# Query and key stacks loaded one head at a time, projections spread between score units, and modulation rows summed on GpSimd

## The reference

```
mod0 = silu(L0_c) @ L0_wmod          # (1,512) @ (512, 3072): shift, scale, gate of each half block
mod1 = silu(L1_c) @ L1_wmod          # the same for block 1
h  = layernorm(x) * (1 + scale) + shift
q  = (h @ Wq.T) -> 32 heads of 16;  k, v = (h @ Wk.T), (h @ Wv.T) -> 8 heads of 16
q, k = rope(q), rope(k)
s  = q k^T / 4, causal over 1024 tokens;  out = softmax(s) @ v;  x = x + gate * (out @ Wo.T)
# then: mlp with top-2 routing, a mixer block, a gated mlp with low-rank terms, each with shift, scale, gate
```

## Time and profile before

| | us |
|---|---|
| median of 3 runs | 860.44 (856.64 to 864.11) |
| the profiled execution | 860.34 |
| its span in the trace | 858.5 |
| mean granted TensorE clock | 0.952 of full |

### The profile page before, as it was taken

The page is one execution under the profiler, slowest core; times in us unless marked ns, Lnnn a source line. Parts: engine busy times, 40 slices in busy tenths (PEclk is TensorE's granted clock), DMA queues, the critical chain, the costliest instruction groups (busy, mean ns, idle before and its releaser), DMA issues.

```text
span 858.5 us, 11485 instructions
## 1 busy us (share of the span) xinstructions
PE 757.5 (88%) x3902; PEld 454.3 (53%) x3902; DVE 471.0 (55%) x714; ACT 322.1 (38%) x532; POOL 204.8 (24%) x158
## 2 busy tenths in 40 slices
PE   5979489999999999979889999877778899997998
PEld 2434233243333433217658888634336688885886
DVE  4636556667667677406855637693686423336310
ACT  6311056555665556771315500253213222322100
POOL 1405560200000000161246513231323122222500
PEclk9979789999999999999999999998779899999999
DMA  9291994510010100211014300110221011111110
GB/s 316 71 147 15 170 175 119 73 63 25 38 62 0 62 28 36 90 38 62 2 29 106 98 1 0 39 54 1 36 54 49 24 50 49 49 31 43 62 62 37
DMA packets 24376, 52.88 MB, mean 62 GB/s; under 512 B 4017, under 2 KB 8857, under 8 KB 23321
## 3 DMA queue, kind: packets, MB, share of 16 engines
q1 hardware_dynamic: 24345, 52.46, 23.6%
HBM read 45.63 MB, written 6.62 MB: 61 GB/s over the span
## 4 chain that ended last, share of the span: by engine, by line
PE 74%; DVE 10%; issue 5%; DMA 4%; ACT 3%; SPq 2%; POOL 2%; ACTq 0%; DVEq 0%; POOLq 0%
PE ps L842 72%; DVE mxp L1691 2%; DMA Qst<-mparts 1%; ACT pr L1395 1%; DVE xnb L1588 1%; PE ps L859 1%; DMA q_parts<-qparts 1%; DMA x<-in_x 1%; DVE st L1566 1%; PE ps L997 1%; DMA Qst<-q_parts 1%; DVE arena L1595 1%; DVE dg L1922 1%; DVE rt L1880 1%; SPq L717 1%
## 5 line engine op out<-in xcount | busy, mean ns | idle before, releaser
L842 PE MATMUL ps<-arena 128*128 128x512 f32 (+1 forms) x1416 | 333.6, 397 | 12.9 <-ACT full L1522 5.4
L842 PEld LDWEIGHTS ps<-arena 128*128 128x128 f32 (+1 forms) x1416 | 266.4, 189 | 74.3 <-DVE arena L1598 11.7
L1691 DVE TENSOR_REDUCE mxp<-ps 128x2 f32<-128x1024 f32 (+3 forms) x160 | 173.2, 1115 | 83.7 <-PE ps L842 83.0
L1395 ACT ACTIVATE pr<-ps 128x512 f32<-128x512 f32 x288 | 161.7, 596 | 126.6 <-PE ps L842 123.9
L842 PE MATMUL ps<-Qst,Kst 99*128 (+1 forms) x288 | 105.7, 388 | 16.8 <-DMA Qst<-mparts 9.4
L842 PE MATMUL ps<-Kst,Qst 96*128 (+4 forms) x384 | 102.7, 340 | 10.0 <-DMA Qst<-q_parts 5.8
L842 PE MATMUL ps<-pr,vr 128*32 128x512 f32 x576 | 77.6, 611 | 0.7 <-ACT pr L1395 0.7
L842 PE MATMUL ps<-maskb,identb 128*128 128x128 bf16 (+1 forms) x320 | 76.2, 260 | 0.0
L842 PEld LDWEIGHTS ps<-Kst,Qst 96*128 (+1 forms) x384 | 37.0, 101 | 73.1 <-issue 40.7
L842 PEld LDWEIGHTS ps<-Qst,Kst 99*128 (+1 forms) x288 | 27.2, 97 | 86.6 <-ACT pr L1395 48.9
L2097 POOL COPY vr<-vtok 128x128 f32 (+1 forms) x8 | 2.3, 291 | 206.1 <-PE ps L842 206.1
(11 more groups left out here) (187 smaller groups left out, 786.0 us busy)
## 6 DMA issues: line engine op xcount, KB each, us to landing
wmr<-in_wmr SPq DMA_DIRECT2D x8, 1280.0 KB, 6.0
raw<-in_w SPq DMA_DIRECT2D x16, 512.0 KB, 3.3
Qst<-q_parts SPq DMA_DIRECT2D x18, 256.0 KB, 8.8
q_parts<-qparts SPq DMA_DIRECT2D x3, 768.0 KB, 8.4
x<-in_x SPq DMA_DIRECT2D x8, 256.0 KB, 6.3
wm<-in_wm SPq DMA_DIRECT2D x4, 512.0 KB, 7.1
raw<-in_up SPq DMA_DIRECT2D x8, 256.0 KB, 2.6
raw<-in_down SPq DMA_DIRECT2D x8, 256.0 KB, 2.6
```

The lines of the kernel that those rows point to most:

```text
L842: return nc.tensor.matmul(outp, lhs, rhs, start=start, stop=stop, skip_group_check=True)
L1395: A(pr[:, k % PRING, :], ps[:, 4 + k % 2, :], ACT.Exp, scale=float(DH) ** -0.5).then_inc(exp_done, 1)
L1691: V.tensor_reduce(mxp[:, kh, g0:g0 + heads, i].rearrange("p (b e) -> p b e", e=per), units, AXX, ALU.max)\
```

## The change

- `Qst` and `Kst` hold three heads instead of eight; head h uses slot h % 3. Nine DMAs load a head: three for the keys (one for each group of rows), six for the queries (64 KB for a half, 128 KB for all tokens). Head h+2's are issued after head h's maxima rows and, from h = 1, after head h-1's transposed units are all done.
- SyncE's order is one plain list: maxima rows of head h, its modulation row, next weights, then (h < 3) the store of query parts h+1, then the loads of head h+2. The first modulation weights are loaded in the front.
- The first queries are projected before the second half of the layer norm is turned. The splitting of the first queries moves to VectorE; the keys' stays on ScalarE, VectorE and GpSimd.
- Values of the second half and query groups 1 and 2 are projected in halves, one behind each of the first ten score units; the transposes of the values follow unit 11, group 3 stands around the first maxima and head 1's first units.
- GpSimd weighs the four chunks of a modulation piece by the conditioning (a number for each partition) and adds them to `wsum`; `mod_step` is then four products with ones.
- The loops over heads are written out on all engines.

```diff
+    if n >= NKV - 2:
         return slots_before(NKV) + 2 * (n - (NKV - 2))
     return slots_before(n + 2, "ctx")
+
+
+FILL = (("v", 1), ("q", 1, 0), ("q", 1, 1), ("q", 2, 0), ("q", 2, 1))
+VT_AT = 11
...
+            sp.dma_start(wmr[:, :, :].rearrange("p c n -> p (c n)"), a["wmr"][0]).then_inc(wmr_in, 16)
+
+            def load_keys(n, tok_, done):
+
+                for r0, parts_ in ((0, 3), (3, 2), (5, 1)):
+                    sp.dma_start(Kst[DH * r0:DH * (r0 + parts_), n % 3, tok_], kscr[0:parts_, DH * n:DH * n + DH, tok_])\
+                        .then_inc(done, 16)
...
+            def load_queries(n, tok_, done):
+
+                r = G * DH * (n % 2)
+                for k, part in enumerate(Q_PARTS):
+                    sp.dma_start(Qst[DH * k:DH * k + DH, n % 3, :, tok_],
+                                 qscr[n // 2, part, r:r + G * DH, tok_].rearrange("(g d) t -> d g t", d=DH)).then_inc(done, 16)
...
-            load_keys(2, NKV, slice(0, T), k_rest)
...
-            def later_queries(c):
-
-                sp.wait_ge(part_q, c)
-                sp.dma_start(qscr[c, :, :, :].rearrange("q p t -> p q t"), qparts[:, :, :]).then_inc(q_out, 16)
-                sp.wait_ge(q_out, 16 * c)
-                load_queries(c, slice(0, T), q_in[c])
...
+                sp.wait_ge(k_lo, hf + 1)
+                sp.dma_start(kscr[:, :, tok[hf]].rearrange("q p t -> p q t"), parts[2 * hf][:, :, :]).then_inc(part_out[2 * hf], 16)
+                sp.wait_ge(q_lo, hf + 1)
+                sp.dma_start(qscr[0, :, :, tok[hf]].rearrange("q p t -> p q t"), parts[2 * hf + 1][:, :, :])\
+                    .then_inc(part_out[2 * hf + 1], 16)
+                sp.wait_ge(part_out[2 * hf], 16)
+                load_keys(0, tok[hf], s0_in[hf])
+                sp.wait_ge(part_out[2 * hf + 1], 16)
+                load_queries(0, tok[hf], s0_in[hf])
+            load_keys(1, every, st_in[1])
+            load_queries(1, every, st_in[1])
+            sp.dma_start(lraw[:, :], a["lora"]).then_inc(lraw_in, 16)
...
                 sp.wait_ge(s_read, slots_before(h, NS + 1) + 1)
-                for blk in range(2):
-                    sp.dma_start(mscr[blk, bass.ds(h * MODW, MODW)].rearrange("(q n) -> q n", n=MODW // 4),
-                                 full[16 * blk:16 * blk + 97:32, 0, 0:MODW // 4]).then_inc(modrow_out, 16)
-                if more:
-                    sp.wait_ge(s_full, slots_before(h, NS + 1) + 1)
-                    sp.dma_start(wmr[:, :, :].rearrange("p c n -> p (c n)"),
-                                 a["wmr"][bass.ds(h + 1, 1)].rearrange("o p n -> (o p) n")).then_inc(wmr_in, 16)
-
-            head_dmas(0, True)
-            later_queries(2)
-            head_dmas(1, True)
-            later_queries(3)
-            sp.dma_start(lraw[:, :], a["lora"]).then_inc(lraw_in, 16)
-            with sp.Fori(0, NKV - 3) as k:
...
-            sp.wait_ge(modrow_out, 32 * NKV)
+                sp.dma_start(mscr[h * MODW:(h + 1) * MODW].rearrange("(q n) -> q n", n=MODW // 4), full[0:97:32, 0, 0:MODW // 4])\
+                    .then_inc(modrow_out, 16)
+                if h < NKV - 1:
+                    sp.wait_ge(wsum_ready, h + 1)
+                    sp.dma_start(wmr[:, :, :].rearrange("p c n -> p (c n)"), a["wmr"][h + 1]).then_inc(wmr_in, 16)
+
+            for h in range(NKV):
+                head_dmas(h)
+                if h < 3:
+                    sp.wait_ge(part_q, h + 1)
+                    sp.dma_start(qscr[h + 1, :, :, :].rearrange("q p t -> p q t"), qparts[:, :, :]).then_inc(q_out, 16)
+                if h < NKV - 2:
+
+                    sp.wait_ge(q_out, 16 * ((h + 2) // 2))
+                    if h:
+                        sp.wait_ge(t_full, h * NTU)
+                    load_keys(h + 2, every, st_in[h + 2])
+                    load_queries(h + 2, every, st_in[h + 2])
...
             pe.wait_ge(wkv_in, 16)
             keys(0)
-            ln_turn(0, 1)
             pe.wait_ge(wq_sorted, KC)
             queries(0, 0)
+            ln_turn(0, 1)
             keys(1)
             queries(0, 1)
             values(0)
-            queries(1, 0)
...
-                pe.wait_ge(wmr_in, 16 * h + 16)
-
+                pe.wait_ge(wsum_ready, h + 1)
                 w = MODW // 4
-                for kc in range(KC):
-                    for q in range(4):
-                        last = mm(ps[32 * q:32 * q + 32, 2, 0:w], sc32[:, kc, :, :].rearrange("p l m -> p (l m)"),
-                                  wmr[:, kc, w * q:w * q + w], kc == 0, kc == KC - 1)
+                for q in range(4):
+                    last = mm(ps[32 * q:32 * q + 32, 2, 0:w], ones[:, 0:32], wsum[:, w * q:w * q + w], True, True)
                 last.then_inc(s_full, 1)
...
+            pe.wait_ge(s0_in[0], 144)
             for s in range(NS):
                 if s == LATER:
-                    values(1)
-                    queries(1, 1)
+                    pe.wait_ge(s0_in[1], 144)
+                s_unit(0, s)
+                if s < 2 * len(FILL):
+
+                    job, half = FILL[s // 2], range(2 * (s % 2), 2 * (s % 2) + 2)
+                    if job[0] == "v":
+                        values(job[1], half)
+                    else:
+                        queries(*job[1:], half)
+                if s == VT_AT:
                     for hf in range(2):
                         values_turn(hf)
-                    pe.wait_ge(k_in[1], 96)
-                    pe.wait_ge(q0_in[1], 96)
-                s_unit(0, s)
-                if s in (7, 10, 13, 16):
-                    queries(*divmod((7, 10, 13, 16).index(s) + 4, 2))
             max_turn(0)
+            queries(3, 0)
             mod_step(0)
+            pe.wait_ge(st_in[1], 144)
             for s in range(AHEAD):
                 s_unit(1, s)
+                if s in (1, 3):
+                    queries(3, 1, range(s - 1, s + 1))
...
-            head_body(0, True, True, False)
-            with pe.Fori(0, NKV - 3) as k:
-                head_body(k + 1, True, True, True)
-            head_body(NKV - 2, True, False, True)
-            head_body(NKV - 1, False, False, True)
+            for n in range(NKV):
+                head_body(n, n < NKV - 1, n < NKV - 2, n > 0)
...
+                n = 2 * hf + 1
+                dve.wait_ge(rope_q, n + 1)
+                V.tensor_copy(parts[n][:, 0, :], rq[n][:, :]).then_inc(q_part, 1)
+                dve.wait_ge(q_part, 3 * hf + 1)
+                V.tensor_tensor(rq[n][:, :], rq[n][:, :], parts[n][:, 0, :], ALU.subtract).then_inc(q_part, 1)
+                dve.wait_ge(q_part, 3 * hf + 2)
+                V.tensor_copy(parts[n][:, 1, :], rq[n][:, :]).then_inc(q_part, 1)
+                dve.wait_ge(q_part, 3 * hf + 3)
+                V.tensor_tensor(parts[n][:, 2, :], rq[n][:, :], parts[n][:, 1, :], ALU.subtract).then_inc(q_lo, 1)
...
+            rope_begin(0)
+            ln_norm(0, 1, range(2))
+            rope_end(0)
+            ln_norm(0, 1, range(2, 4))
+            key_rest(0)
+            rope_begin(1)
+            rope_end(1)
+            query_parts(0)
+            dve.wait_ge(trig_in[1], 32)
+            rope_begin(2)
+            rope_end(2)
+            rope_begin(3)
+            key_rest(1)
+            rope_end(3)
+            query_parts(1)
...
-                if s == 12:
-                    swap_queries(2)
-            swap_queries(3)
+                if s in (8, 14):
+                    swap_queries(1 + (8, 14).index(s))
...
+            swap_queries(3)
+            for n in range(NKV - 1):
+                if n == 1:
+                    dve.wait_ge(part_q, 3)
+                head_body(n, True, n < NKV - 2, n > 0)
...
+            def weigh(h):
+
+                pool.wait_ge(wmr_in, 16 * h + 16)
+                if h:
+                    pool.wait_ge(s_full, slots_before(h - 1, NS + 1) + 1)
+                else:
+                    pool.wait_ge(c_silu, 1)
+                split_at = min(max(2048 - h * MODW, 0), MODW)
+                for l, (n0, n1) in enumerate(((0, split_at), (split_at, MODW))):
+                    if n0 == n1:
+                        continue
+                    for kc in range(KC):
+                        c_ = sc32[:, kc, l, 0:1]
+                        to = wmr[:, kc, n0:n1] if kc else wsum[:, n0:n1]
+                        link(nc.gpsimd.tensor_scalar(to, wmr[:, kc, n0:n1], c_, 0.0, ALU.mult, ALU.add))
+                        if kc:
+                            ins = nc.gpsimd.tensor_tensor(wsum[:, n0:n1], wsum[:, n0:n1], to, ALU.add)
+                            if kc < KC - 1 or n1 < MODW:
+                                link(ins)
+                ins.then_inc(wsum_ready, 1)
...
             head_v(0)
+            weigh(0)
             rope_queries(2)
+            weigh(1)
             rope_queries(3)
             head_v(1)
+            weigh(2)
...
+            for n in range(2, NKV):
+                head_v(n)
+                if n < NKV - 1:
```

(1 more changed line is left out.)

292 lines of the change are left out of this document (113 added, 179 removed).

## The result

The changed kernel takes **854.8 us** (median of 20 runs, 850.6 to 859.6) beside 859.7 for the kernel before (20 runs, 856.6 to 865.1). The ratio is 0.9936 with a 95% interval of [0.992, 0.9951]: a gain of 4 to 7 us. It is real, and smaller than the 1% that the forecast set as its bound. The forecast was 857 (847 to 869), with 0.56 on "within 1%".

A forecast was written before the change was run, and what follows sets the result against it. TensorE was taken to bound the kernel, standing still in the front. Chain +0.9, half clock +1.7 and fewer products -6.0 sum to -3.4 us against 860.34, forecast 857 us, range 847 to 869.

The forecast's parts named there:

- -1.0 us a head: TensorE's modulation step: four products instead of sixteen save 1.0 us a head, -6.0 us for heads 2 to 7.
- The weighing, 8.4 us: GpSimd's new four scalings and three additions take 8.4 us a head, bounds 7.8 and 10.0; hidden in later heads.
- the rival of a slower GpSimd: Weighing above 8.4 us costs double on the serial chain: 860.1 us at 10.0, 870 at 15; chance 0.10.
- The first score: First score product on TensorE in the front at 44.6 us, bounds 41 and 48.4, instead of 48.38.
- The chain of stores and rounds: Heads 0 and 1: serial query stores, GpSimd rounds and weighings turn 14.5 us of lead into +0.9 us.
- The wait of 13.2 us before the context transposes: TensorE, there at 135.2, stands 13.2 us until 148.4 for VectorE, which waited for GpSimd's third round.
- The half clock after it, +1.7: TensorE's clock at half rate after the long stand before the context transposes costs 1.7 us.
- The lock: VectorE's maxima of heads 0 and 1 finish with GpSimd's weighing; without that, head 0's chain is 1.5 us shorter.
- Sum: Whole kernel: +0.9 + 1.7 - 6.0 = -3.4 us, giving 857 us.
- shorter chain: Stores land in 6.4 us, first score 2 us sooner, no lock or half clock: 849 us; chance 0.28.
- Straight code costs: Five looped bodies become straight and TensorE must fetch instructions, 3 us a body: 872 us; chance 0.08.
- The four products save nothing: TensorE would wait for VectorE's scores at the same place instead: 863 us; chance 0.06.

The follow-up runs named there:

- e3: The kernel before with the attention heads' loops written out on all engines and nothing else: 859.3 us, ratio 0.9995.
- e1: The changed kernel with SyncE storing the second and third rounds of query parts as soon as they are made: 845.2 us, ratio 0.9845.
- e2: The changed kernel without GpSimd's weighing, the sixteen modulation products per head back on TensorE: 857.6 us, ratio 0.9968.
- e8: The changed kernel with early query stores, later mask copy, later VectorE wait, and GpSimd's third round held until head 1's maxima steps finish: 838.1 us.
- e5: The changed kernel with VectorE's copy of the causal mask moved behind the second half's statistics: 853.5 us, ratio 0.9928.
- e7: e1 with GpSimd's weighing removed and the sixteen modulation products per head back on TensorE: 851.7 us, ratio 0.9899.

## Why the prediction was right, step by step

- **What bounds it.** TensorE in the steady heads, the waits in the front: yes. 16 products became 4 and the steady head fell as forecast, to 34.69 us (34.7 forecast).
- **-1.0 us a head.** Right in size, in part by luck, as two errors cancel. Measured are 0.81 for the products (1.29 to 0.48, where I had put the four at 0.3) and 0.23 for the straight code (35.73 to 35.50 in e3), which I had priced at nothing. In the last interval of value copies only 0.24 came (30.87 to 30.63).
- **The weighing, 8.4 us.** Exact: scalings of 0.80 and additions of 1.54 (0.85 and 1.5 forecast). The groups by shape on GpSimd after, as in the earlier trace rows:

```profile
L2100 POOL TENSOR_TENSOR wsum<-wsum,wmr 128x640 f32<-128x640 f32 x21 | 32.3, 1539 | 1.8
L2098 POOL TENSOR_SCALAR wmr<-wmr,sc 128x640 f32<-128x640 f32 x21 | 16.8, 799 | 2.0
```

  The row of like width was the right guide, not the one of like form; the rival of a slower GpSimd (0.10) did not come.
- **The first score.** 42.58 against 44.6. The store left 1.1 us later than forecast (35.29, behind the mask), but only 7.3 us passed from it to the first product, not 10.4. I had also given 3 us to a lower clock after it, as in the earlier trace rows. The clock was 1.00 from 42.58 to 50.00: TensorE had idled 1.60 us before, not 5.79. The lower clock came later, 0.59 in 71.20 to 83.64, where the weighing hid it. With both, head 0's modulation product came 4.9 us sooner than forecast (83.64, forecast 88.5), and its transposed scores at 90.80, not 95.7.
- **The chain of stores and rounds**, link by link, forecast in brackets: store issued 86.68 (92.1), landed after 8.5 (8.4), second round made 109.2 (114.4), weighed 117.5 (122.8), product 119.48 (122.8), store issued 122.79 (124.7), landed after 9.2 (8.4), third round made 145.9 (147.1), transposes 147.25 (148.4). The order of the links is right and GpSimd's have their length, but three are longer than forecast, and they take 4.3 of the 5.4 us by which the chain began early. **The one that failed**: TensorE was to arrive at head 1's product at 118.3, 22.6 us after head 0's start, and stand for GpSimd. It took 28.7 us, 4.6 more than the 24.07 of before, and GpSimd was done 2.0 us ahead of it. In those 28.7 us TensorE idles 4.3, against 1.4 before. It stands 1.33 us (95.23) for a reduction that came behind two swaps of query halves on VectorE, 0.72 each, and 2.15 us, not 1.20, for negated maxima that took VectorE 1.14 us beside the weighing (0.19 for head 0). The other 1.7 us are work at a lower clock: 24.39 us at a mean of 0.87, where before it was 22.65 at 0.91; the forecast had counted this way at full clock. Second, the store went out 3.3 us behind the product and not 1.9: head 1's maxima rows left only at 119.44 and took 1.82 us of the queue ahead of it, for which the forecast had no term. Third, the landing took 9.2, not 8.4. So the 4.9 us of lead shrank to 1.2 without changing what ended the chain.
- **The wait of 13.2 us before the context transposes**: 13.93, released by VectorE's reduction that itself stood 15.81 us for GpSimd's round. e1 removes it by the queue's order alone; e2 shows that the weighing did not make it. The forecast's remark that each microsecond of weighing costs two was too dear: GpSimd had 2 us to spare at head 1, and in e2 the whole weighing, less the products that replace it, is worth 0.8 us from store to store.
- **The half clock after it, +1.7.** Present (0.50 in 147.25 to 151.00), and right in size. From the first context transposes to the third value copy the changed kernel takes 36.23 us (to 183.48); with a clock of 1.00 there, e8 takes 34.43 (129.22 to 163.65) and e1 33.99 (139.74 to 173.73). That is 1.8 to 2.2 us.
- **The lock.** The forecast let the maxima of head 0 finish with the weighing. They did. VectorE's five steps of head 0, after:

```profile
79.05 0.28 DVE L1699 TENSOR_SCALAR mt<-ps 32x128 f32<-32x128 f32 x1 [0.56 <-PE ps L937]
79.36 0.21 DVE L1701 CAST mparts<-mt 32x128 bf16<-32x128 f32 x1
79.61 1.50 DVE L1702 TENSOR_TENSOR mt<-mt,mparts 32x128 f32<-32x128 f32 x1
81.15 0.79 DVE L1703 CAST mparts<-mt 32x128 bf16<-32x128 f32 x1
81.98 1.66 DVE L1704 TENSOR_TENSOR mparts<-mt,mparts 32x128 bf16<-32x128 f32 x1
```

  They end at 83.6, with the weighing at 83.5. TensorE did not wait for it there: with one whole projection in front, it came to the product at 83.64. That is luck: the projection took 4.89 us at the lower clock (3.60 at full clock), without which TensorE would have stood about 1 us, an estimate from these two rows; the forecast had 1.5.
- **Sum.** Forecast -3.4, measured -4.9. By the traces the transposes stand at -0.2 (forecast +0.9), and the last value copy at -3.8 (354.38 against 358.17). That this is near -3.4 is partly luck. Between the second and the third copy the changed kernel gains 0.1 us (37.60 against 37.67), where +1.7 for the clock less 1.0 was forecast, since the kernel before met a lower clock there too (as told for e3). One later head took 36.20 us (287.55 to 323.75) instead of 34.69, at a clock of 0.66 in 310 to 315. And the last interval gave 0.24, not 1.0. The remaining -1.7 of the profiled pair lies behind attention, where both kernels do the same work; the other kernels' stretches there vary more, from 499.0 us (e2) to 504.5 (e5). So no part of the forecast's sum accounts for it.

The rivals: *shorter chain* did not hold, as the stores landed in 8.5 and 9.2 us, not 6.4, and the lock and the half clock both came. *Straight code costs* falls with e3. *The four products save nothing* falls with 34.69 and e2's 35.50. Where the expected lead went is now shown, not argued: 19.4 us at head 0's start, given back on a chain through SyncE's queue and GpSimd. e8 recovers most of it: its context transposes start at 129.22, 18.3 us ahead of the kernel before.

## What to carry to other kernels

When a step is brought forward, follow what its queue issues behind it to the next engine's start. Here the lead ran into stores that stood behind the very rows that had been moved ahead; issuing them first was worth 9.6 us, more than the whole change. Time taken off an engine ahead of its long wait is swallowed by it: the products of heads 0 and 1 were worth nothing that can be told, those of the steady heads 0.81 us each. When two medians differ by just the sum that was expected, look in the traces for the place: for e7 half of the profiled pair's difference lay elsewhere. And short steps on VectorE that others wait for should not run beside long GpSimd instructions; a wait that keeps the two apart can make the kernel faster.

## What the hardware showed that I had not expected

VectorE's short steps beside GpSimd, by kind, alone and at worst: a subtraction with two SBUF operands 0.28 and 2.45 us; a cast from SBUF to SBUF 0.21 and 2.32; two reductions from PSUM, of 1024 and 768 columns, take 2.09 with GpSimd idle (after, at 122.98) and 2.09 beside its third round (e8, at 119.04). So in these rows the loss goes by what the step reads, and lasts until GpSimd's instruction ends. The Trainium skill (SBUF — State Buffer, section "SBUF: two separate sides") says this of steps in a two-port mode or with two SBUF inputs: whichever starts first keeps the shared ports for its whole instruction. The forecast left open whether the casts are held too; e1's rows of 1.58 and 2.32 us show that they are.

The straight heads are 0.23 us shorter than the looped ones, and cost nothing in all. And TensorE's clock does not go by the length of one stand. It stayed at its full level after 1.60 us at 42.58 and was at the lower one after 5.79 and after 13.93. But it was also 0.50 in 95 to 100, after 1.33 us at 95.23 in a stretch in which TensorE had worked 2.46 of 4.20 us; and behind nearly equal stands it was low in e2 (3.17 us) and full in the changed kernel (3.33). What decides it no run here shows.
